# Half of the LSTM's input steps gathered as x rows and multiplied, half as finished gate rows

## The reference, cut to what matters

```python
b = bih + bhh
def step(carry, x_t):                    # x_t = x[src] of this step: (512, 128)
    h, c = carry
    g = x_t @ wih.T + h @ whh.T + b      # (512, 512): gates i, f, g, o
    i, f, gg, o = jnp.split(g, 4, axis=-1)
    c = sigmoid(f) * c + sigmoid(i) * tanh(gg)
    h = sigmoid(o) * tanh(c)
    return (h, c), None
...
h1  = relu(lstm(x[src]) @ wl.T + bl + x @ wr.T)      # conv 1
out = lstm(h1[src]) @ wl.T + bl + h1 @ wr.T          # conv 2
x   = layernorm(x + out)
x   = layernorm(x + rgcn(x, weight, edge_weight, src, dst, edge_type_3))   # one message per edge, summed at dst
```

## Time and profile before

| | us |
|---|---|
| runs shown, median (lowest, highest) | 576.14 (573.68, 580.67) |
| span of the profiled execution | 570.4 |
| median of the runs less that span | 5.7 |
| layer 0 of the LSTM, its h products end | at 213.2 |
| layer 1, its h products from and to | 230.0 to 422.4 |
| messages, sum and last layer norm | 422.4 to 570.4 |

### The profile page before, as it was taken

How to read it: one execution, slowest core, us unless ns; L and a number is a source line. 1 busy time by engine, 2 the same in 40 slices (tenths; PEclk the granted TensorE clock), 3 DMA queues, 4 the chain that set the end, 5 groups by cost and what they waited for, 6 DMA issues and landing times.

```text
span 570.4 us, 9783 instructions
## 1 busy us (share of the span) xinstructions
PE 485.2 (85%) x3463; PEld 349.4 (61%) x3463; DVE 399.5 (70%) x1114; ACT 325.8 (57%) x832; POOL 309.4 (54%) x320
## 2 busy tenths in 40 slices
PE   8766998979897999778897888887899987978795
PEld 4644786757676785656666766775785543444343
DVE  5544887858676895557776776876787975757665
ACT  4734766737556674545565665655675664545543
POOL 6476565665546501676664566666204655656551
PEclk9997999979999999978989999999999999999899
DMA  5665665675646502665665456556202111111111
GB/s 191 204 188 168 180 192 159 177 195 161 175 125 197 166 11 93 187 180 161 172 169 148 134 163 183 167 169 181 77 1 79 48 38 38 42 38 41 39 42 29
DMA packets 28346, 72.85 MB, mean 128 GB/s; under 512 B 6795, under 2 KB 10691, under 8 KB 28298
## 3 DMA queue, kind: packets, MB, share of 16 engines
q0 software_dynamic: 20768, 64.77, 40.0%
q1 hardware_dynamic: 6442, 6.54, 4.0%
q10 hardware_dynamic: 1088, 0.92, 0.5%
HBM read 69.05 MB, written 3.16 MB: 127 GB/s over the span
## 4 chain that ended last, share of the span: by engine, by line
PE 39%; DVE 17%; ACT 16%; another core or an unknown queue 13%; issue 8%; DMA 6%; POOL 1%; DVEq 0%; ACTq 0%; POOLq 0%
PE gates L1254 18%; DMA edge_rows<-msg_table,msg_index 6%; PE gates L1247 5%; PE work L1254 4%; DVE msg_full L1090 3%; ACT act_if L601 3%; ACT h_hi L597 3%; DVE prod_fc L906 2%; DVE prod_ig L908 2%; ACT msg_full L750 2%; PE work L1247 2%; DVE h_full L877 2%; ACT act_o L619 2%; ACT tanh_c L593 2%
## 5 line engine op out<-in xcount | busy, mean ns | idle before, releaser
L524 POOL DMA_INDIRECT rows<-gate_table,src_steps x226 | 224.7, 994 | 165.1 <-issue 64.5
L1247 PE MATMUL gates<-ident,rows 128*128 128x128 f32 x686 | 99.5, 281 | 39.5 <-issue 20.8
L601 ACT ACTIVATE act_if<-gates 128x512 f32<-128x512 f32 x113 | 67.8, 600 | 104.1 <-remote 54.5
L539 POOL DMA_INDIRECT edge_rows<-msg_table,msg_index x76 | 75.5, 993 | 79.6 <-DMA msg_table<-table_sb 30.9
L1254 PE MATMUL gates<-h_hi,whh_hi 128*128 128x256 f16 x396 | 104.7, 283 | 13.1 <-ACT h_hi L597 6.6
L906 DVE TENSOR_TENSOR prod_fc<-act_if,cell 128x256 f32<-128x256 f32 x128 | 54.2, 424 | 81.3 <-issue 37.3
L1247 PEld LDWEIGHTS gates<-ident,rows 128*128 128x128 f32 x686 | 78.1, 144 | 52.1 <-issue 49.7
L1254 PE MATMUL gates<-h_hi,whh_lo 128*128 128x256 f16 x396 | 104.1, 281 | 0.0
L1254 PE MATMUL gates<-h_lo,whh_hi 128*128 128x256 f16 x396 | 88.1, 282 | 0.4 <-issue 0.4
L890 DVE TENSOR_TENSOR h_lo<-h_full,h_hi 128x256 f16<-128x256 f32 x128 | 54.2, 423 | 12.3 <-ACT h_hi L597 0.9
L1080 DVE TENSOR_SCALAR rows<-node_iota,dst_f 128x512 f16<-128x512 f16 x132 | 43.4, 365 | 26.8 <-ACT msg_full L750 25.7
(11 more groups left out here) (186 smaller groups left out, 800.5 us busy)
## 6 DMA issues: line engine op xcount, KB each, us to landing
rows<-gate_table,src_steps POOLq DMA_INDIRECT x226
gate_table<-rows SPq DMA_DIRECT2D x8, 256.0 KB
edge_rows<-msg_table,msg_index POOLq DMA_INDIRECT x76
code<-code_table SPq DMA_DIRECT2D x6, 160.0 KB
msg_table<-table_sb SPq DMA_DIRECT2D x4, 192.0 KB, 2.4
code<-code_table SPq DMA_DIRECT2D x5, 128.0 KB
whhT<-turned_whh SPq DMA_DIRECT2D x2, 256.0 KB
wihT<-turned_wih ACTq DMA_DIRECT2D x1, 256.0 KB, 2.9
```

What stands on the lines that cost most here:

```text
L524: pool.indirect_dma_start(rows[:, j * K + k, :], None, gate_table[l], bass.IndirectOffsetOnAxis(src_steps[:, t, k:k + 1], axis=0)).then_in ...
L539: pool.indirect_dma_start(edge_rows[:, c % 2, n, :], None, msg_rows, bass.IndirectOffsetOnAxis(msg_index[:, pool_first(c) + n:pool_first(c ...
L601: act.activation(act_if[:, h, :], gates[:, h, 0, :], ACT.Sigmoid, scale=1 / G_SCALE).then_inc(if_ready[h], 1)
L1247: pe.matmul(gate_place(t, h, gate)[:, k * P:(k + 1) * P], rows[:, j * K + 2 * h + k, gate * P:(gate + 1) * P], ident[:, :], is_transpose=True,
```

## The change

`MODES` gives each step of each layer a letter: X (x rows of 512 bytes are gathered, turned and multiplied), G (gate rows of 2048 bytes from the table) or P (one-hot, now only the first two steps of layer 1). X and G alternate, so that 30 steps come from the tables instead of 57, and 34 steps are gathered as x rows. For an X step POOL gathers four tiles of 128x128, PE turns them with four products (`turn_rows`) one step ahead, ACT takes the high part and DVE the low part (`take_x`), PE multiplies them by `wih` (24 products) and ACT adds the bias. Layer 1's x rows are those of h1, so DVE now also writes h1 to `h1_rows` and SP stores it to `h1_table`. X rows and gate rows have a ring of five steps each. Most of the one-hot machinery goes: `spread_src`, `take_src`, three of the five one-hot matrices, the middle `gather_x` calls. Smaller moves: 18 warm-up products instead of 9, the table projections of layer 0 in one block before the first turned rows, those of layer 1 in one block behind `turn_x`, the loads of x_nodes and of the one-hot index rows (now broadcast, 512 KB) on SP, one product with xT_biased moved to the end of layer 1.

In the diff below the pieces are, in order, the constants, SP between the layers, POOL's gathers, `take_x` of ACT (called ahead of i and f of the step before its own), `take_x` of DVE (called behind the low part of h 1, ahead of the cell products of half 0 of the step before its own), and PE's loop over the steps.

```diff
-WARM = 9
-DIRECT = (1, 2, 12)
-HALF = 21
+WARM = 18
+STEPS = 33
+MODES = ("XXX" + "GX" * 15, "PP" + "XG" * 15 + "X")
...
+            for h in range(2):
+                sp.wait_ge(h1_rows_ready, h + 1)
+                sp.dma_start(h1_table[h * HN:(h + 1) * HN, :].rearrange("(k p) c -> p k c", p=P),
+                             h1_rows[:, 2 * h:2 * (h + 1), :]).then_inc(h1_stored, 16)
...
+            issued = [(l, t, k) for l, t in fetched for k in range(K)]
+            for l, t in fetched:
+                by_x_row = MODES[l][t] == "X"
+                if by_x_row:
+                    turn = by_x.index((l, t))
+                    if turn >= XDEEP:
+                        pool.wait_ge(rows_turned, 2 * (turn - XDEEP + 1))
+                    if l == 1 and by_x[turn - 1][0] == 0:
+                        pool.wait_ge(h1_stored, 32)
+                else:
+                    turn = by_rows.index((l, t))
+                    if turn == 0 or by_rows[turn - 1][0] != l:
+                        pool.wait_ge(table_stored, 16 * K * (tabled.index(l) + 1))
+                    if turn >= DEEP:
+                        pool.wait_ge(gates1[1], steps_done(*by_rows[turn - DEEP]))
                 for k in range(K):
-                    if issued.index((turn, k)) >= UNDER_WAY:
-                        landed, tile = issued[issued.index((turn, k)) - UNDER_WAY]
-                        pool.wait_ge(rows_in[landed % DEEP * K + tile], 16 * rows_count(landed, tile))
-                    pool.indirect_dma_start(
-                        rows[:, j * K + k, :], None, gate_table[l],
+                    at = issued.index((l, t, k))
+                    if at >= UNDER_WAY:
+                        pool.wait_ge(*landing(*issued[at - UNDER_WAY]))
+                    target, table = ((x_rows[:, x_slot(l, t, k), :], (x, h1_table)[l]) if by_x_row
+                                     else (rows[:, row_slot(l, t, k), :], gate_table[l]))
...
+            def take_x(l, t):
+                i = x_turn(l, t)
+                if MODES[l][t] == "X":
+                    act.wait_ge(rows_turned, 2 * (by_x.index((l, t)) + 1))
+                    act.activation(xg_hi[:, i % 2, :], row_bank[i % 2], ACT.Copy, scale=X_SCALE).then_inc(xg_hi_ready, 2)
...
+                i = x_turn(l, t)
+                if MODES[l][t] == "X":
+                    dve.wait_ge(xg_hi_ready, 2 * (i + 1))
+                    dve.scalar_tensor_tensor(xg_lo[:, i % 2, :], row_bank[i % 2], X_SCALE, xg_hi[:, i % 2, :],
+                                             op0=ALU.mult, op1=ALU.subtract).then_inc(xg_lo_ready, 2)
...
                 for t in range(1, T):
-                    if picked_half(l, t, 0):
-                        picked_first(t, 0)
-                        picked_second(t, 0)
-                    else:
-                        gathered_first(t, 0)
-                        gathered_second(t, 0)
-                    if t + 1 in BY_ONEHOT:
-                        gather_x(l, BY_ONEHOT.index(t + 1))
...
+                    input_first(t, 0)
+                    input_second(t, 0)
+                    if t + 1 < T and MODES[l][t + 1] == "X":
+                        turn_rows(l, t + 1)
+                    input_first(t, 1)
+                    input_second(t, 1)
                     recurrent(t, 0, l * (T - 1) + t)
-                    if picked_half(l, t, 1):
-                        picked_second(t, 1)
                     recurrent(t, 1, l * (T - 1) + t)
```

More of the change, by code:

```diff
@@ L63, in build_program, with steps_of, of_x, x_turn @@
     HN = N // 2
[L64 to L84, removed]
+    DEEP, XDEEP = 5, 5
+    PICKED = 2
+    def steps_of(modes):
+        return [(l, t) for l in range(2) for t in range(T) if MODES[l][t] in modes]
+    by_rows, by_x, from_x = steps_of("G"), steps_of("X"), steps_of("XP")
+    fetched = steps_of("GX")
+    tabled = [l for l in range(2) if "G" in MODES[l]]
+    SLOTS = DEEP * K if by_rows else 12
+    def of_x(l, t):
+        return MODES[l][t] in "XP"
+    def x_turn(l, t):
+        return from_x.index((l, t))
+    def x_slot(l, t, k):
+        return by_x.index((l, t)) % XDEEP * K + k
+    def x_fills(l, t):
+        return by_x.index((l, t)) // XDEEP + 1
+    def row_slot(l, t, k):
+        return by_rows.index((l, t)) % DEEP * K + k
+    def row_fills(l, t):
+        return by_rows.index((l, t)) // DEEP + 1
     TILES = E // P
@@ L310, in build_program @@
         table_stored = sem("table_stored")
-        rows_in = [sem(f"rows_in{s}") for s in range(SLOTS)]
+        landed = [sem(f"landed{s}") for s in range(DEEP * K)]
         gates0 = pair("gates0")
@@ L422, in table_owner, with landing @@
             return 0 if k in (0, 3) else 1
[L424 to L430, removed]
+        def landing(l, t, k):
+            turn = fetched.index((l, t))
+            return landed[turn % DEEP * K + k], 16 * (turn // DEEP + 1)
         def steps_done(l, t):
@@ L987, in _ @@
                 if l == 0:
-                    take_x(0, 2)
+                    take_x(0, 1)
                 for t in range(1, T):
                     now, step = l * T + t + 1, l * (T - 1) + t
-                    spare = [s for s in range(DIRECT[1] + 6, T) if s not in DIRECT]
+                    spare = [s for s in range(8, T) if s != 12]
                     if l == 1 and t in spare[:K * PICK_PIECES[1]]:
@@ L1221, in _ @@
-            add_bias(0, 1, last=True).then_inc(projected, 1)
-            pe.wait_ge(src_rows_ready, 1)
-            spread_src(2)
-            project(0, xT, 2, first=True)
-            add_bias(0, 2, last=True).then_inc(projected, 1)
+            if 0 in tabled:
+                pe.wait_ge(x_loaded, 16)
+                pe.wait_ge(bias_ready, 2)
+                for k in range(K):
+                    add_bias(0, k, first=True)
+                    project(0, xT, k, last=True).then_inc(projected, 1)
@@ L1226, in _ @@
             pe.wait_ge(ident_ready, 2)
             turn_rows(0, 0)
-            project(0, xT, 3, first=True)
-            add_bias(0, 3, last=True).then_inc(projected, 1)
-            turn_rows(0, 1)
             pe.wait_ge(wih_hi_ready, 1)
@@ L1305, in gathered_first @@
                     for k in (2 * h, 2 * h + 1):
[L1306 removed]
+                        pe.wait_ge(*landing(l, t, k))
                     pe.wait_ge(if_ready[h], l * T + t)
```

386 lines of the change are left out of this document (151 added, 235 removed).

## The result

The changed kernel takes 667.5 us (median of 4 runs, 666.1 to 669.2) beside 574.9 for the kernel before: a ratio of 1.159, interval 1.151 to 1.166. I had forecast 560. The profiled execution has a span of 667.4 us, where the sum gave 553.9.

What follows compares the result with a forecast made beforehand. PE was taken as near its limit, delayed by late updates and locked with POOL. Layer 0 205.7, between layers 18.0, layer 1 182.0, the rest 148.0 and 0.2 gave a 553.9 us span; with 5.7 around it 560, range 530 to 591.

Steps and rivals of the forecast that it cites:

- the clean step: In the LSTMs, a table step undisturbed by gathers takes 4.43 us, with no hole on PE.
- the late updates: Beside gathers of 2048-byte rows, PE's semaphore updates reach ACT late, at a present price of 1.6 us per four large gathers.
- the lock of POOL and PE: In layer 1, PE's update waits for POOL's burst of four gathers, and the next burst waits for that update.
- the pace of the whole layer: In layer 1 of the kernel before, bursts of four gathers begin 5.98 us apart, taken as the pace throughout.
- Price of a pair: An X step and a G step together, without late updates: 5.3 and 5.0, so 10.3 us against 12.0 before.
- the covers of the low and high parts of x: In a G step, ACT's and DVE's added work lengthens the ring to 5.1 us, still under PE's 5.28.
- the ring of an X step: The loop through ACT and DVE back to PE's h products takes 5.0 us and binds, since PE needs 4.85.
- So the lock opens: POOL no longer waits for PE, PE's stalls no longer delay gathers; POOL's 10.4 to 11.0 us a pair is close below.
- So I charge the large ones alone: Only groups of four large gathers hold PE's updates, 1.2 us each: 15 x 1.2 = 18 us a layer.
- the range from 0.7 to 1.6: Bounds in us on the late-update charge per group of four large gathers, giving 545 to 575 us in total.
- The first: Rival: small gathers hold PE's updates as large ones do, 34 x 1.2 = 41 us, so 601 us; chance 0.14.
- The third: Rival: POOL binds above PE as small gathers wait for large ones' landings; pairs of 12.0 us, 572 to 578; chance 0.10.

Runs made afterwards that it cites:

- e1_lead5: Changed kernel with POOL made to wait for PE so that it is at most five fetched steps ahead, not ten; 621.5 us, ratio 1.083.
- e8_g_small: e3_all_g with gathers of G steps behind the first five fetching rows of 512 bytes in place of 2048; 599.7 us, ratio 1.021.
- e9_g_two: e3_all_g with two gathers of 256 KB, not four, in each G step behind the first five; 508.6 us, ratio 0.866.
- e2_all_x: Changed kernel with every gathered step of kind X, so only rows of 512 bytes are gathered; 612.8 us, ratio 1.065.
- e3_all_g: Changed kernel with every gathered step of kind G behind the first three (two in layer 1); 596.3 us, ratio 1.031.
- e12_drain: Changed kernel with POOL waiting, at the first ten steps of each layer, until the step before's gathers have landed; 700.2 and 712.0 us.
- e15_space256: Changed kernel with a memset of 128x256 on POOL behind each gather of the recurrences; 640.1 us, ratio 1.090.
- e17_space512: Changed kernel with a memset of 128x512 of 16-bit values on POOL behind each gather; 634.5 us, ratio 1.077.
- e16_before_space512: Kernel before with a memset of 128x512 on POOL behind each gather of the recurrences; 583.3 us, ratio 0.997.

## Why the prediction was wrong

**What bounds the kernel.** Right: the clean step, the late updates beside gathers, the lock of POOL and PE. Read too evenly: 5.98 us is not "the pace of the whole layer" but near the mean of steps that took from 4.43 to 10.63 us. And not read far enough: the earlier trace rows begins at 47 us, and the earlier trace rows are from later still. The stretch that decided is at the layers' starts, where step 3's h products came 16 us before step 4's in the kernel before, and PE stood still while POOL filled its ring of five steps.

**Price of a pair.** 10.3 forecast, 10.09 measured. Right, and so were the covers of the low and high parts of x: the halves are 5.28 and 4.81 us, what PE's own products need, so the ring of an X step, put at 5.0, does not bind.

**POOL.** The failed step is this one: "POOL no longer waits for PE: it would have to be ten steps ahead. So the lock opens". POOL does get ten steps ahead, at the start of each layer, because the same hold stops PE for as long as POOL fills its rings. It cost 46.8 us in layer 0 (step 4's h products at 86.1, by the sum at 39.3) and 45.6 in layer 1: 92 of the 113 us between sum and span. The lock with POOL had bounded the hold in the kernel before. e1_lead5 says how much of this goes with the depth of ten: held to five, step 4 of layer 0 comes 33 us earlier, and steps 1 to 3 of layer 1 take 21.2 us in the place of 56.5 (by the sum 10.3). The other 14 and 11 us are the hold beside a run of five steps' gathers, which the kernel before had as well and the sum did not charge there.

**"So I charge the large ones alone".** Wrong in its reason. The hold goes with the number and spacing of gathers (e8_g_small, e9_g_two), and e2_all_x has it with small ones alone. The eight small gathers at the start were weak evidence: updates pass now and then in the long runs too, as at 284.90. Its size was off too, and the range from 0.7 to 1.6 had been made narrower than its own ends of 0 and 1.6: 19 steps from 86.1 to 208.2 took 6.43 us each, a pair of 12.9, or 2.8 over the clean pair and not 1.2; the ten steps of the tail had no hold at all. The two nearly made up for each other, which was luck: layer 0 from step 4 on took 171.6 us for a forecast of 166.4, layer 1 from step 2 on 184.4 for 176.7. The Trainium skill's rule that I had set against this (DMA: Bandwidth & Descriptors, section Bandwidth: 64 KB takes 0.95 us, smaller transfers are bound by descriptors) decides nothing here. It gives the span in which one transfer keeps the DMA engines at work, and my 0.29 us was the mean busy time of one DMA engine, so the two need not disagree as I had said; and a fall of the DMA share from 0.64 to 0.21 (e3_all_g, e8_g_small) changed nothing.

**The sum's small terms.** Between the layers 21.6 for 18.0, the messages 4.6 more than taken.

**Rivals.** The first (small gathers hold too, 601) had the right cause and was priced as a constant loss per group, 41 us, where it was a standstill of ring length. The third (POOL binds, pairs of 12.0) comes near the stretches with gathers in its number, a pair of 12.9, but not in its cause: from 86.1 to 211 us POOL waited 16.1 us for PE's gates and 6.2 for large rows to land, and no wait of PE is put down to rows. It is the lock again, ten steps deep. None had the starts, and so the range ended at 591.

## What to carry to other kernels

Where a producer queue runs ahead of an engine that it disturbs, the depth of its ring is not free: the disturbed engine stands still until the ring is full, falls that far behind, and pays the whole depth as a tail when the producer has finished. Before deepening a ring, look at the layer's first steps in the trace, not at its steady middle, and measure from the last transfer to the end of the work. And a small idle gap between gathers may be worth more than it costs: 0.2 us more behind each was worth 5 per cent in the kernel before, and 0.4 us more nothing.

## What the runs showed of the hardware

- PE's semaphore updates were late by up to 37 us (e12_drain; 21.8 in the changed kernel) while POOL issued gathers of 128 rows 1.25 us apart. Nothing like it is seen from ACT to DVE: the two sigmoids from 298.28 end at 299.12, DVE's product starts at 299.15, and PE's matmul at 299.26. What inside the chip holds the updates is not visible in these records and stays open.
- In the kernel before, the hold depends on the gap between gathers (0.30, 0.39, 0.50, 0.7 us: 54.5, 42.6, 23.1, 0 us of waits of one instruction group); in the changed kernel 0.5 us is too little (e15_space256, 90 us of such waits) and 0.7 enough (e17_space512, none). It does not depend on bytes (181 or 56 GB/s: the same pace).
- A memset on POOL between gathers (0.33 us for 128x256, 0.55 for 128x512) does not hold PE's updates: with the longer one, ACT's i and f have no "remote" wait in the recurrences (e16_before_space512, e17_space512).
- With PE busy for 10 of 51 us, its granted clock fell to 0.55 (279.3 to 330.2 us), near the lower of its two levels, 1.2 GHz; products of 256 columns in that stretch started 0.21 us apart and not 0.11, as at 299.43 and 299.64.
